# Attention of four gated layers: keys, queries and maxima dealt to stack rows through memory, batches streamed without stages, and in block 0 the clip of the probabilities on GpSimd

## The chip, the cores and the metric

The kernel runs on one core of one Trainium2 chip. The metric is the device time of one execution in microseconds (us). The core has a matrix engine (TensorE, PE), a vector engine (VectorE, DVE), a scalar engine (ScalarE, ACT), a general engine (GpSimd, POOL) and a queue for transfers (SyncE, SP); POOL's queue can issue transfers as well. The engines run their own instruction lists and wait for each other through semaphores.

## The reference, cut to what matters

`x` is 4 batches x 256 tokens x 256 features (D), the context 4 x 512 x 256. Four layers follow each other, each an attention part and a feed-forward part (FFN):

```
x = x + tanh(g_xattn[0]) * L0_xattn(layernorm(x), ctx, mask)   # "block 0": 16 heads of 16
x = x + tanh(g_ffn[0])   * L0_ffn(layernorm(x))                # 8 experts
x = x + tanh(g_xattn[1]) * L1_xattn(layernorm(x), ctx)         # "memory": one head, no weights
x = x + tanh(g_ffn[1])   * L1_ffn(layernorm(x))
x = x + tanh(g_xattn[2]) * L2_xattn(layernorm(x), ctx)         # "block 2": 16 heads, int8 queries
x = x + tanh(g_ffn[2])   * L2_ffn(layernorm(x))                # sign weights
x = x + tanh(g_xattn[3]) * L3_xattn(layernorm(x), ctx, lens)   # "block 3": two softmaxes
x = x + tanh(g_ffn[3])   * L3_ffn(layernorm(x))                # 16 experts
```

Attention of block 0, per batch and head:

```
q, k, v = x @ Wq.T + bq, ctx @ Wk.T + bk, ctx @ Wv.T + bv      # split in 16 heads of 16
scores  = clip(q @ k.T / 4, -50, 50);  masked keys get -50
probs   = softmax(scores);  probs = probs / (sum(probs) + 1e-8)
out     = layernorm(res_scale * ((probs @ v) @ Wo.T + bo)) * gamma + beta
```

Block 2 quantizes its input and its attention output to int8 by the row's largest value; block 3 normalizes queries and keys by their root mean square and has one softmax over the 257 image keys and one over the text keys, whose results are added. Blocks 2 and 3 subtract each row's maximum ahead of the exponential.

## The kernel before, in words

**Precision.** Every fp32 factor of a product is split in a high and a low part, and PE makes three passes (high x high, low x high, high x low). For the scores the parts stand in one "stack" of 64 rows per head: 16 rows of the high part, 16 of the low, 16 of the high again, and 16 for masks and maxima; two heads (a pair) fill the 128 rows. One matmul over the stack does all passes of a score.

**Stacks by turning.** Tokens are projected with tokens on the partitions (`kv`, `q`; the matmuls are at L370). ACT copies the high parts into `stack_k` or `stack_q` (L719), DVE the low parts (L899). PE turns the stack by matmuls with an identity, eight 128x128 for 128 tokens (`turn_stacks`, L541; "tk" for keys, "tq" for queries), and ACT (L750) and DVE (L1057) copy the result out of PSUM into `keys` and `queries`, two buffers each. In blocks 2 and 3 queries are turned a second time ("re") once the maxima stand in the stack (L912, L914).

**Work on a pair.** A unit is one head and 256 keys: `scores` (L596) makes two matmuls of 256 columns into one of two PSUM banks; ACT takes the exponential of 128x512 (L728). 32 units make a batch. In block 0 DVE clips four units' exponentials, 128x2048, to e^-50 and e^50 (L1013; 8 per batch). `weigh` (L634) multiplies by the values, 8 or 12 instructions per four units, each of four passes on fp32. `maxima` (L610) makes a 128x512 product per head and 128 tokens in three banks that the projections use too, and DVE reduces it (L1025 in block 2, L1022 and L1023 in block 3): 32 products per batch.

**The order.** `order` writes down one list of steps, and every engine follows it. It is cut in stages: stage s holds the projections and turns of batch s, the scores of batch s-1 spread over them, the finish of batch s-2 (`dt`, `ot`, `wo`), and at its end the maxima of batch s. Costs in `COST` only set how scores are spread. Blocks 2 and 3 start the scores of a stage after "neg" and "re", which need all maxima of the batch. There are 6 stages for 4 batches. POOL does roots (L765), zeroes the unused halves of `queries` (L783), and splits some weights and contexts.

Of the kernel before, what the change touches and what calls it, by code (L numbers as in the profile page):

```python
# [81 lines left out]
PARTS = 2 * G  # L82


def stage_steps(s, peak):
# [1976 lines left out]
```

How the kernel before makes its waits and increments, by code:

```python
    def wait(eng, kind, n):  # L349
        if isinstance(n, int) and n <= 0:
            return
        eng.wait_ge(sems[kind], n)
# [1 line left out]
    def link(eng, name, ins):  # L355
        chain[name] += 1
        ins.then_inc(sems[name], 1)
        eng.wait_ge(sems[name], chain[name])
# [26 lines left out]
        def w(eng, kind, n):  # L386
            if n > 0:
                eng.wait_ge(sems[kind], n + before_attention("pw" if kind[:2] == "pw" else kind, blk))
# [85 lines left out]
            def kv(b, kt):  # L475
                if b == 0 and kt == 0:
                    if blk == 0:
                        eng.wait_ge(sems["w0_l"], 1)
                        eng.wait_ge(sems["bias_l"], 2)
                    elif blk == 2:
                        eng.wait_ge(sems["w2_l"], 2)
                    else:
                        eng.wait_ge(sems["w3_l"], 6)
                if blk == 0 and kt == 0:
                    eng.wait_ge(sems["ct_l" if b else "ct_l0"], max(b, 1))
                wait_proj_free(eng, b, kt)
# [3 lines left out]
                        mats[m_] = [[(mi, P)], [(mi, P)], [(m_, P), (mi, 1)], [(m_, P)]][kt]  # L490
                lhs = lambda m: ctx_cols(b, kt * P, kt * P + m)
                dst = place(b, kt)
                project(mats[WK], dst, lhs)
                if blk == 0 and b == 0 and kt == 0:
                    eng.wait_ge(sems["w0_l"], 2)
                bank = PROJ_BANKS[(5 * b + PROJ_USE[kt]) % 3]
                then(project(mats[WV], psum[:, bank, D:2 * D], lhs), "pj_full")
# [1405 lines left out]
        def masks():  # L1903
            eng.wait_ge(sems["d_small"], 16 * 5)
```

## Time and profile before

| | |
|---|---|
| time, median of 3 | 1501.76 us (1501.28 to 1501.77) |
| profiled execution | 1505.82 us, span of its trace 1504.0 us |
| mean granted TensorE clock | 0.868 |
| PE busy | 1235.6 us (82%) |
| DVE busy | 868.8 us (58%) |
| ACT busy | 598.5 us (40%) |
| POOL busy | 190.3 us (13%) |
| DMA | 37.16 MB, mean 25 GB/s |

Busy times are sums over the span; every number after this one is on the trace's own clock, which begins at 0 and ends at 1504.0. Block 0 lies from 0 to 262.6, the FFNs and the memory attention to 594.6, block 2 to 886.9, its FFN to 934.0, block 3 to 1257.3, and the last FFN to the end. "Granted clock" is the share of 2.4 GHz that TensorE ran at; a stretch at 0.5 runs at 1.2 GHz.

### The profile page before, as it was taken

Reading aid. Unit: us, or ns where it says so; the run is one execution under the profiler, and the core shown is the slowest. Engines: PE = TensorE matmul, PEld = TensorE weight load, DVE = VectorE, ACT = ScalarE, POOL = GpSimd, SP = SyncE. Lnnn points to the kernel's source line nnn. Section 1 sums busy time; section 2 is a strip of 40 time slices with the busy share of each in tenths; the row PEclk is TensorE's granted clock in tenths of the full one; section 3 lists DMA queues with packets and bytes.
Section 4 is the critical chain, followed back from the end, with each engine's and each line's share of the span. In section 5 each row is a group of like instructions: output and inputs, shape, how many; then the busy total and the mean of one; then the engine's idle time right before and its main releaser. Section 6 shows DMA issues by size and latency. Waiting matters only on the chain. (4 is left out here: it accounts for less than half of the span.)

```text
span 1504.0 us, 21057 instructions
## 1 busy us (share of the span) xinstructions
PE 1235.6 (82%) x7698; PEld 981.6 (65%) x7698; DVE 868.8 (58%) x1890; ACT 598.5 (40%) x1161; POOL 190.3 (13%) x213
## 2 busy tenths in 40 slices
PE   3887874899856997688888767788888876999998
PEld 3765642788745886565656545565757556888887
DVE  6455465455567456667586656567474724555555
ACT  3555642233222232234535533335545351333332
POOL 6000001222101122000000030300001001222221
PEclk8898886799968899569889889769798986999999
DMA  3000001111010010000000020000000001111111
GB/s 128 1 1 1 1 1 58 67 49 49 22 51 14 25 56 6 0 1 1 1 1 1 1 84 25 1 1 1 1 1 1 1 1 38 49 49 53 57 49 40
DMA packets 17925, 37.16 MB, mean 25 GB/s; under 512 B 2341, under 2 KB 7734, under 8 KB 17850
## 3 DMA queue, kind: packets, MB, share of 16 engines
q1 hardware_dynamic: 17690, 36.14, 7.6%
q8 instruction: 48, 0.79, 0.2%
q14 instruction: 27, 0.22, 0.1%
q0 software_dynamic: 160, 0.01, 0.0%
HBM read 35.10 MB, written 1.05 MB: 24 GB/s over the span
## 5 line engine op out<-in xcount | busy, mean ns | idle before, releaser
L728 ACT ACTIVATE probs<-psum 128x512 f32<-128x512 f32 x384 | 218.1, 600 | 188.9 <-PE psum L596 183.2
L596 PE MATMUL psum<-queries,keys 128*128 128x256 f32 x768 | 170.0, 329 | 25.4 <-ACT probs L728 25.1
L1406 DVE TENSOR_TENSOR ff_hl<-ff_h,ff_hh 128x512 fp32r<-128x512 f32 x114 | 108.4, 951 | 139.5 <-ACT ff_hh L1263 139.5
L370 PE MATMUL psum<-ff_xh,ff_wh 128*128 128x512 f32 x424 | 171.1, 404 | 2.1 <-DVE ff_xl L1378 1.4
L596 PEld LDWEIGHTS psum<-queries,keys 128*128 128x128 f32 x768 | 128.6, 212 | 67.5 <-ACT probs L728 53.4
L370 PE MATMUL psum<-ff_xl,ff_wh 128*128 128x512 f32 x424 | 169.6, 400 | 0.0
L1287 ACT ACTIVATE ff_s<-psum 128x512 f32<-128x512 f32 x98 | 58.7, 599 | 250.5 <-PE psum L370 250.5
L370 PE MATMUL psum<-ff_xh,ff_wl 128*128 128x512 f32 x392 | 154.9, 395 | 0.0
L610 PE MATMUL psum<-keys,queries 128*128 128x512 f32 x256 | 126.1, 554 | 19.8 <-DVE negmax L1025 10.1
L370 PE MATMUL psum<-ff_wh,ff_hh 128*128 128x256 f32 x456 | 128.3, 286 | 7.8 <-DVE ff_hl L1406 7.7
L634 PE MATMUL psum<-probs,values 128*32 128x256 f32 x1664 | 124.4, 427 | 9.0 <-DVE probs L1013 6.6
L370 PE MATMUL psum<-ff_wh,ff_hl 128*128 128x256 f32 x456 | 126.8, 283 | 0.0
L370 PE MATMUL psum<-ff_wl,ff_hh 128*128 128x256 f32 x392 | 110.9, 283 | 0.0
L541 PE MATMUL psum<-ident_r,stack_k 128*128 128x128 f32 x384 | 67.4, 327 | 48.9 <-DVE stack_k L899 40.6
L610 PEld LDWEIGHTS psum<-keys,queries 128*128 128x128 f32 x256 | 54.1, 222 | 76.2 <-DVE negmax L1025 34.3
L370 PEld LDWEIGHTS psum<-ff_wh,ff_hh 128*128 128x128 f32 x456 | 86.8, 190 | 18.1 <-DVE ff_hl L1406 13.3
L1388 DVE TENSOR_TENSOR ff_s<-ff_s,psum 128x512 f32<-128x512 f32 x98 | 66.8, 682 | 54.5 <-PE psum L370 54.5
L541 PEld LDWEIGHTS psum<-ident_r,stack_k 128*128 128x128 f32 x384 | 60.9, 239 | 56.2 <-DVE stack_k L899 46.0
L370 PEld LDWEIGHTS psum<-ff_xh,ff_wh 128*128 128x128 f32 x424 | 82.5, 194 | 17.3 <-DVE ff_xl L1378 1.8
L370 PEld LDWEIGHTS psum<-ff_xl,ff_wh 128*128 128x128 f32 x424 | 82.4, 194 | 13.2
L370 PE MATMUL psum<-w_hi,ctx_hi 128*128 128x256 f32 x208 | 68.8, 331 | 23.0 <-DVE bias L1898 12.8
L370 PEld LDWEIGHTS psum<-ff_wh,ff_hl 128*128 128x128 f32 x456 | 86.9, 191 | 0.1
(246 smaller groups left out, 2419.5 us busy)
## 6 DMA issues: line engine op xcount, KB each, us to landing
ff_raw<-in_ff SPq DMA_DIRECT2D x49, 448.0 KB, 3.3
w_raw<-in_w SPq DMA_DIRECT2D x12, 256.0 KB, 4.4
ff_raw<-in_ff SPq DMA_DIRECT2D x8, 256.5 KB, 2.7
ct_raw<-in_ctx_t SPq DMA_DIRECT2D x4, 512.0 KB, 7.5
cn_raw<-in_ctx SPq DMA_DIRECT2D x4, 512.0 KB, 5.2
x<-in_x SPq DMA_DIRECT2D x4, 256.0 KB, 7.4
out<-x SPq DMA_DIRECT2D x8, 128.0 KB, 1.8
w_nat<-in_w_nat SPq DMA_DIRECT2D x1, 512.0 KB, 5.5
```

The source lines that it names most:

```text
L370: last = eng.matmul(dst, lhs[i](k), rhs[j](k), start=start and n == 0, stop=stop and n == groups * len(pairs) - 1, skip_group_check=True)
L541: last = eng.matmul(psum[:, bank, j * P:(j + 1) * P], src[:, 4 * h + j, :], ident_r[:, :], start=True, stop=True, skip_group_check=True)
L596: last = eng.matmul(psum[:, n % 2, i * S:(i + 1) * S], kst[c % 2][:, h // 2, kt * P:(kt + 1) * P], qst[c % 2][:, h % 2, h // 2, :], start= ...
L610: last = eng.matmul(psum[:, PROJ_BANKS[n % 3], :], qst[b % 2][:, h % 2, h // 2, qt * P:(qt + 1) * P], kst[b % 2][:, h // 2, :], start=True ...
L634: last = eng.matmul(psum[32 * j:32 * j + 32, 4, col:col + S], values[:, c % 2, slot, h * VW:h * VW + 32], probs[:, n % 3, j, kt * S:(kt + ...
L728: then(eng.activation(probs[:, n // 4 % 3, u % 4, :], psum[:, n % 2, :], ACT.Exp, scale=SCALE), "p_exp")
L1287: then(eng.activation(ff_s[:, hf, :], psum[:, 4 + hf, :], ACT.Silu), "f_sd")
L1388: then(eng.tensor_tensor(ff_s[:, hf, :], ff_s[:, hf, :], psum[:, 6, :], ALU.mult), "f_td")
L1406: then(eng.tensor_tensor(ff_hl[:, hf, :], ff_h[:, hf, :], ff_hh[:, hf, :].bitcast(F32), ALU.subtract), "f_hr")
```

## The change

- Keys are projected already turned in blocks 0 and 2 (`kt`: features on partitions, 512 keys in a row, six matmuls of 512 columns per half); the weights' columns are put in a fitting order on the host, and the bias comes with ACT's copy (`bias_c`). Block 3 projects two tiles of tokens into one bank (`kp`) and turns them with four transposes (`tk`); queries of blocks 2 and 3 likewise (`tq`).
- High and low parts go to `keys_turned` and `queries_turned`. SP writes them to DRAM (`keys_out` 3 x 512 KB per batch, `queries_out` 3 x 256 KB), and POOL's queue reads them back into the stack rows, in two halves of 8 heads each (`kr`, `qr`: four pieces of 48 rows x 8 KB, four of 64 rows x 4 KB per batch). The constant rows come from DRAM once per buffer; the mask of block 0 is the exponential's bias.
- Maxima are reduced into `nmx`, cast, turned by one matmul per half (`nt`), written to DRAM and read into the query rows (`nr`); no second turning of the queries.
- A unit is one pair and 128 keys, one matmul of 512 columns. Block 0 has three score banks.
- No stages: `order` gives each step a position counted in units, over all batches; blocks 2 and 3 make one maximum per unit, and its scores come 23.5 units later (`LAG`).
- In block 0 POOL clips (`cl`), and DVE no longer does.

```diff
-COST = {"kv": 2.0, "xt": 0.8, "neg": 0.5, "re": 1.8, "kn": 0.3, "st": 0.6, "tk": 1.7, "q": 1.5, "dt": 1.0,
-        "ot": 0.8, "tq": 1.8, "ln": 0.8, "wo": 1.2, "mx": 1.25, "early": 4.0}
...
-        if peak and s < B:
-            stage += [("mx", s, h) for h in range(NH)]
...
+LAG = 23
+SCORE_BANKS = {0: (0, 1, 2), 2: (0, 1), 3: (0, 1)}
...
+        if peak:
+            for k in range(UNITS_OF_BATCH):
+                at(r + k, "mx", c, k)
...
+        for u in range(UNITS_OF_BATCH):
+            at(r + u + lag + .5, "sc", c, u)
+        for part in range(PARTS):
+            if not peak:
+                at(r + 4 * part + 3 + 1.4, "cl", c, part)
...
+            def keys_turned(st):
...
+                then(passes(eng, bank(st), parts(WK, slice(m * P, (m + 1) * P)), ctx_cols(b, 0, M)), "b_full")
...
-                    for j in range(4):
-
-                        last = eng.matmul(psum[:, bank, j * P:(j + 1) * P], src[:, 4 * h + j, :], ident_r[:, :],
-                                          start=True, stop=True, skip_group_check=True)
...
-                for i in range(2):
-                    kt = 2 * (part % 2) + i
-                    last = eng.matmul(psum[:, n % 2, i * S:(i + 1) * S],
-                                      kst[c % 2][:, h // 2, kt * P:(kt + 1) * P],
-                                      qst[c % 2][:, h % 2, h // 2, :], start=True, stop=True,
-                                      skip_group_check=True)
...
+                dst = psum[:, score_banks[n % len(score_banks)], :].rearrange("p (h c) -> p h c", c=S)
+                then(eng.matmul(dst, kst[buf(c)][:, pair, kt * P:(kt + 1) * P], qst[buf(c)][:, :, pair, :],
+                                start=True, stop=True, skip_group_check=True), "st_full")
...
+            def keys_in(b, ph):
+                wait_buffer(b, ph)
+                eng.wait_ge(sems["d_kw"], written(b))
+                pairs = slice(JJ * ph, JJ * (ph + 1))
+                for m in range(2):
+                    src = kd[b, m, :, :, pairs, :].rearrange("s r j c -> (s r) j c")
+                    move(kst[buf(b)][64 * m:64 * m + AUG, pairs, :], src, f"d_r{buf(b)}{ph}")
...
+            def clip(c, part):
+
+                n = PARTS * c + part
+                w(eng, "p_exp", 4 * (n + 1))
+                pr = probs[:, n % 3, :, :, :].rearrange("p k j c -> p (k j c)")
+                then(eng.tensor_scalar(pr, pr, EXP50N, EXP50P, ALU.max, ALU.min), "p_done")
...
+            def keys_out(b):
+                w(eng, "lo_done", plan.count["lo_done", ("te" if two else "ke", b, 1)])
+                for slot, half in enumerate((1, 0, 1)):
+                    move(kd[b, :, slot].rearrange("m r j c -> (r j) m c"), kt_st[:, :, half, :].bitcast(F32), "d_kw")
```

PE's list before, in block 2 when batch 1 is prepared (L541 are turns, L596 scores of batch 0, L610 maxima of batch 1, L634 weighted sums):

```order
L541 MATMUL psum<-ident_r,stack_k 128x128 x8
L596 MATMUL psum<-queries_60,keys_52 128x256 x4
L610 MATMUL psum<-keys_53,queries_61 128x512 x2
L596 MATMUL psum<-queries_60,keys_52 128x256 x2
L610 MATMUL psum<-keys_53,queries_61 128x512 x2
L634 MATMUL psum<-probs,values 32x256 x8
L596 MATMUL psum<-queries_60,keys_52 128x256 x2
L610 MATMUL psum<-keys_53,queries_61 128x512 x4
L596 MATMUL psum<-queries_60,keys_52 128x256 x2
L610 MATMUL psum<-keys_53,queries_61 128x512 x2
L596 MATMUL psum<-queries_60,keys_52 128x256 x4
```

and after, in the same block (L688 are maxima, L679 scores, L712 weighted sums, L632 turns the maxima):

```order
L712 MATMUL psum<-probs,values 32x256 x8
L688 MATMUL psum<-keys_53,queries_60 128x512
L679 MATMUL psum<-queries_60,keys_53 128x512
L688 MATMUL psum<-keys_53,queries_60 128x512
L679 MATMUL psum<-queries_60,keys_53 128x512
L688 MATMUL psum<-keys_53,queries_60 128x512
L679 MATMUL psum<-queries_60,keys_53 128x512
L688 MATMUL psum<-keys_52,queries_59 128x512
L679 MATMUL psum<-queries_60,keys_53 128x512
L712 MATMUL psum<-probs,values 32x256 x8
L632 MATMUL psum<-ident_r,nm_hl 128x128
```

The turns are gone, a unit's scores are one instruction, and maxima alternate with scores one to one over the whole batch, also across its end.

DVE's list before at the same place, the batch's maxima (L1025) in one piece:

```order
L826 RECIPROCAL small<-small 128x1
L827 TENSOR_SCALAR xn<-xn,small 128x256
L828 TENSOR_SCALAR xn<-xn 128x256
L1057 CAST keys_53<-psum 128x4x128
L1025 TENSOR_REDUCE negmax<-psum 128x1 x32
L952 TENSOR_SCALAR xt_hi<-psum 128x512
L912 CAST stack_q<-negmax 128x16 x2
L914 TENSOR_TENSOR stack_q<-negmax,stack_q 128x16 x2
L1057 CAST queries_61<-psum 64x4x128 x2
```

and after (L1139 are the maxima; L1023 to L1036 the norm of a coming batch's input):

```order
L1139 TENSOR_REDUCE nmx<-psum 128x1 x12
L1023 BN_STATS stat<-x 128x6 x2
L1026 BN_AGGR mv<-stat 128x2 x2
L1028 TENSOR_SCALAR ve<-mv 128x2
L1139 TENSOR_REDUCE nmx<-psum 128x1 x2
L1036 TENSOR_SCALAR xn<-x,mv,rstd 128x256 x2
L1003 TENSOR_REDUCE small<-xn 128x2
L1004 TENSOR_SCALAR small<-small 128x2
L1005 RECIPROCAL small<-small 128x2
L1007 TENSOR_SCALAR xn<-xn,small 128x256 x2
L1010 TENSOR_SCALAR xn<-xn 128x512
L1139 TENSOR_REDUCE nmx<-psum 128x1 x2
```

The 32 reductions now come in pieces with the norm, the key parts and the small casts between them.

POOL's list before, block 0 (L783 zeroes, L765 roots, L1157 the norm ahead of the FFN):

```order
L765 ISA
L765 TENSOR_TENSOR rstd<-ve,half_neg 128x2
L1828 TENSOR_TENSOR ctx_lo<-ct_raw,ctx_hi 128x2x512 x3
L783 MEMSET queries_60 64x2048
L783 MEMSET queries_61 64x2048
L783 MEMSET queries_60 64x2048
L783 MEMSET queries_61 64x2048
L765 TENSOR_TENSOR rstd<-ve,half_neg 128x2 x6
L1157 TENSOR_TENSOR rstd<-ve,half_neg 128x6
```

and after, part of block 0 (L944 are clips, L897 reads back keys and queries, L888 roots):

```order
L944 TENSOR_SCALAR probs<-probs 128x2048 x5
L888 TENSOR_TENSOR rstd<-ve,half_neg 128x2
L944 TENSOR_SCALAR probs<-probs 128x2048 x4
L897 DMA keys_53<-keys_out 48x2048 x2
L897 DMA queries_60<-queries_out 64x1024 x2
L888 TENSOR_TENSOR rstd<-ve,half_neg 128x2
L944 TENSOR_SCALAR probs<-probs 128x2048
L897 DMA keys_53<-keys_out 48x2048 x2
L897 DMA queries_60<-queries_out 64x1024 x2
L944 TENSOR_SCALAR probs<-probs 128x2048 x3
```

Clips stand between the transfers' issues and the roots; a transfer that waits for its data holds what is behind it.

## Rows read from the trace of the kernel before

**Rows 1.** Windows: stretch, us; busy PE, PEld, DVE, ACT, POOL; clock; DMA share, GB/s.
```profile
0.00:262.60 262.60, 182.03 (x1370) 139.80 (x1370) 143.72 (x306) 125.79 (x240) 32.04 (x35) 0.84 0.08 27
262.60:594.60 332.00, 286.52 (x1558) 249.18 (x1558) 186.39 (x379) 103.88 (x191) 55.66 (x57) 0.89 0.12 39
594.60:886.90 292.30, 229.89 (x1482) 166.01 (x1482) 191.49 (x427) 124.82 (x238) 12.91 (x12) 0.81 0.02 5
886.90:934.00 47.10, 36.91 (x198) 28.70 (x198) 31.34 (x50) 16.69 (x41) 11.19 (x11) 0.90 0.19 57
934.00:1257.30 323.30, 263.75 (x1778) 190.47 (x1778) 186.67 (x533) 142.56 (x297) 29.22 (x52) 0.84 0.01 4
1257.30:1504.00 246.70, 236.53 (x1312) 207.43 (x1312) 129.21 (x200) 84.78 (x154) 49.29 (x49) 0.96 0.15 47
```
**Rows 2.** Windows: one batch's stage in block 2, a later one, one in block 3.
```profile
657.70:715.60 57.90, 49.40 (x357) 35.38 (x357) 37.38 (x80) 31.45 (x59) 0.70 (x1) 0.90 0.00 1
776.00:836.20 60.20, 51.75 (x380) 37.58 (x372) 41.05 (x86) 30.76 (x59) 0.00 (x0) 0.91 0.00 1
999.00:1065.00 66.00, 56.12 (x426) 41.49 (x426) 42.89 (x125) 37.04 (x78) 5.39 (x13) 0.92 0.00 1
```
**Rows 3.** One line's instructions: L912, L728, L1013 (min/median/max ns; starts).
```profile
L912 DVE CAST stack_q<-negmax x16: 173/176/184, 657.7 to 1196.4; 128x16 fp32r<-128x16 f32 x8, 128x32 fp32r<-128x32 f32 x8
...
L728 ACT ACTIVATE probs<-psum x384: 579/597/667, 50.7 to 1238.7; 128x512 f32<-128x512 f32 x192
...
L1013 DVE TENSOR_SCALAR probs<-probs x32: 1215/1227/1228, 53.6 to 239.1; 128x2048 f32<-128x2048 f32 x32
```
**Rows 4.** Page, costliest groups: exponentials (L728), turns (L541).
```profile
L728 ACT ACTIVATE probs<-psum 128x512 f32<-128x512 f32 x384 | 218.1, 600 | 188.9 <-PE psum L596 183.2
...
L541 PE MATMUL psum<-ident_r,stack_k 128*128 128x128 f32 x384 | 67.4, 327 | 48.9 <-DVE stack_k L899 40.6
```
**Rows 5.** Timeline of PE: turns, scores, weighted sums.
```profile
659.36 1.01 PE L541 MATMUL psum<-ident_r,stack_q 128*128 128x128 f32 x8
...
1234.52 0.74 PE L596 MATMUL psum<-queries,keys 128*128 128x256 f32 x4
...
1237.11 1.07 PE L634 MATMUL psum<-probs,values 128*32 128x256 f32 x16
```
**Rows 6.** Chain of waits in FFN3: 12 matmuls of 512 columns, 12 of 256.
```profile
1402.72 4.18 PE psum L370 x24
```
**Rows 7.** Groups of DVE in 657.7 to 715.6 (block 2).
```profile
L1025 DVE TENSOR_REDUCE negmax<-psum 128x1 f32<-128x512 f32 x32 | 19.6, 683 | 3.0 <-PE psum L610 3.0
L1057 DVE CAST queries<-psum 64x512 fp32r<-64x512 f32 x8 | 5.5, 687 | 5.5 <-PE psum L541 5.4
L1057 DVE CAST keys<-psum 128x512 fp32r<-128x512 f32 x4 | 2.8, 690 | 2.2 <-PE psum L541 2.2
```
**Rows 8.** Timeline of DVE: first maxima of block 2 and of block 3.
```profile
633.53 19.22 DVE L1025 TENSOR_REDUCE negmax<-psum 128x1 f32<-128x512 f32 x32
...
972.45 0.41 DVE L1022 TENSOR_REDUCE negmax<-psum 128x1 f32<-128x257 f32 x1
```
**Rows 9.** Groups of POOL over the program.
```profile
L783 POOL MEMSET queries<- 64x2048 f32 x12 | 21.6, 1829 | 0.3
...
L1836 POOL CAST w_hi<-w_raw 128x512 fp32r<-128x512 f32 x8 | 5.5, 684 | 0.1
```
**Rows 10.** DMA of 0 to 50 us (16 engines' share); issues of the page.
```profile
q1 hardware_dynamic: 3624, 4.82, 28.8%
...
ct_raw<-in_ctx_t SPq DMA_DIRECT2D x4, 512.0 KB, 7.5
```
**Rows 11.** Timeline near 15 us and at 971 us: DVE L844, POOL L1828.
```profile
15.22 4.81 DVE L844 TENSOR_SCALAR xn<-x,mv,rstd 128x256 f32<-128x256 f32 x2 [0.84 <-POOL rstd L765]
...
971.20 0.73 DVE L844 TENSOR_SCALAR xn<-x,mv,rstd 128x256 f32<-128x256 f32 x2 [0.82 <-POOL rstd L765]
...
15.18 7.08 POOL L1828 TENSOR_TENSOR ctx_lo<-ct_raw,ctx_hi 128x1024 fp32r<-128x1024 f32 x3
```

More of the change, by code:

```diff
@@ new lines, in token_pair @@
+            def token_pair(st, mat, img):
+                _, b, i = st
+                if b == 0 and i == 0:
+                    wait_weights(mat)
+                wait_bank(eng, st)
+                for k in range(2):
+                    kt = 2 * i + k
+                    mats = [(mat, P)]
+                    if two:
+                        mats = [[(img, P)], [(img, P)], [(mat, P), (img, 1)], [(mat, P)]][kt]
+                    last = project(mats, bank(st)[:, k * D:(k + 1) * D],
+                                   lambda m: ctx_cols(b, kt * P, kt * P + m))
+                then(last, "b_full")
@@ new lines, in keys_hi @@
+            def keys_hi(st):
+                _, b, i = st
+                if b and i == 0:
+                    eng.wait_ge(sems["d_kw"], written(b - 1))
+                if blk != 3:
+                    fill = ("kt", b, i)
+                    filled(eng, fill)
+                    then(eng.activation(kt_st[:, i, 1, :], bank(fill), ACT.Identity, bias=key_bias(i)), "hi_done")
+                else:
+                    fill = ("tk", b, i)
+                    copy_hi(st, fill, kt_st[:, :, 1, 2 * P * i:2 * P * (i + 1)],
+                            bank(fill).rearrange("p (m c) -> p m c", m=2))
@@ new lines, in turned_lo @@
+            def turned_lo(st, fill, hi, lo):
+                flat = lambda t: t[:, :, :].rearrange("p c t -> p (c t)")
+                if blk == 2:
+                    wait_readers(eng, st, ("q", "wo"))
+                    filled(eng, fill)
+                    ins = eng.tensor_scalar(flat(hi), bank(fill), -127.0, None, ALU.max)
+                else:
+                    w(eng, "hi_done", plan.count["hi_done", st])
+                    ins = less(flat(lo), bank(fill), flat(hi))
+                then(ins, "lo_done")
@@ new lines, in divide @@
+                dst = o if part == 0 else o_tmp[:, :].rearrange("p (h c) -> p h c", c=HD)
+                spread = inv.rearrange("p (h one) -> p h one", one=1).to_broadcast([P, NH, HD])
+                ins = eng.tensor_tensor(dst, got[:, :, 0:HD], spread, ALU.mult)
+                then(ins, "dt_done")
+                w(eng, "dt_done", plan.count["dt_done", st])
+                last = qt == QT - 1 and part == nparts - 1
+                if blk == 2 and last:
+                    then(quantize(o_n, o_slot(b)), "on_done")
+                elif two and part == 1:
+                    ins = eng.tensor_tensor(o_n[:, qt, :], o_n[:, qt, :], o_tmp[:, :], ALU.add)
+                    if last:
+                        then(ins, "on_done")
@@ L1999, in units @@
         return m.transpose(1, 0, 2).reshape(D, -1)
+    turned = np.array([(2 * j + m) * HD + r for m in range(2) for r in range(HD) for j in range(NP)])
     arrays = {}
```

1283 lines of the change are left out of this document (713 added, 570 removed), and 17 rows, old and new, of the table PREP.

## The prediction, as put on record before the changed kernel ran

> **What bounds the kernel now.** I read first the windows of the whole program [rows 1]. The attention parts of blocks 0, 2 and 3 take 262.6, 292.3 and 323.3 us, together 878.2 of 1504.0. The rest (332.0 + 47.1 + 246.7 = 625.8 us) keeps its arithmetic, so I leave it as it is. In the attention parts PE is busy for 69%, 79% and 82%, at a granted clock of 0.84, 0.81 and 0.84; the last FFN, where PE is busy for 96% of the window, has 0.96. DVE is busy for 55%, 66% and 58% there, ACT for less than half. PE is the main engine, but something else stops it.
>
> Next one batch at a time. The casts of the maxima (L912) of block 2 start at 657.7 and the last batch's at 836.2: (836.2 - 657.7)/3 = 59.5 us per batch; in block 3 (1196.4 - 999.0)/3 = 65.8; in block 0 first exponential to last clip is (239.1 - 50.7)/4 = 47.1 [rows 2, 3]. A stage of block 2 holds 49.4 to 51.8 us of busy PE at clock 0.90 and 0.91, one of block 3 56.1 at 0.92 [rows 2]; the sum of the instructions at full clock is 42 and 48 us (below), so a batch takes 1.4 times what its matmuls need. The page says why: exponentials (L728) were idle for 188.9 us behind PE's scores, and the turns (L541) for 48.9 us behind the stacks that ACT and DVE fill [rows 4]. Last, the maxima stand in one piece: 32 reductions in 19.22 us, 0.60 us each, in the first batch of block 2 [rows 8], during which PE can't run ahead by more than three banks.
>
> **Unit prices at full clock.** Eight turning matmuls 1.01 us; four score matmuls of 256 columns 0.74 by the record, of which the last's end is modelled; 16 records of weighted sum 1.07 [rows 5]. 12 matmuls of 512 columns and 12 of 256 take 4.18 us [rows 6]: by columns 0.232 and 0.116 us each.
>
> **Part 1, PE.** Per batch of block 2 before: maxima 32 x 0.232 = 7.4, scores 64 x 0.116 = 7.4, sums 8 x 1.07 = 8.6, turns 64 matmuls (32 for keys, 16 + 16 for queries) in 8 groups x 1.01 = 8.1, projections 72 x 0.116 = 8.3, transposes 16 and the like 2.2: 42. After: the 8.1 are gone, four transposes (0.5) and two small turns of maxima (0.2) come, scores are 32 x 0.232 = 7.4 as before, and the keys' bias matmuls (4) go: 34. Block 3 by the same count: 48 before; after -8.1 + 1.5 = 41.5. Block 0 has 48 turns per batch (6.1 us): 34 before, 27.5 after. Over 12 batches that is 85 us less of PE. Scores become half as many instructions with the same columns, which I cost at nothing for PE: their columns set their time; the semaphores halve.
>
> **Part 2, DVE and ACT.** In block 2 DVE loses 12 copies of 0.69 us per batch (8 of queries, 4 of keys) [rows 7] and about six low parts of 0.4, and gets three of 0.69 and two small casts: 41.05 - 8.3 - 2.5 + 2.7 = 33 us per batch; block 3: 42.9 - 8.1 = 35 [rows 2]. That stays under PE. In block 0 the clip goes: 8 x 1.227 = 9.8 us per batch [rows 3]. ACT loses copies likewise and stays near 25 us per batch. What hid the reductions in block 2's end-of-stage piece, nothing, is replaced by one reduction per unit beside a score and an exponential (0.60) [rows 3].
>
> **Part 3, the trip through memory.** Per batch 1536 KB of keys go out and 1536 KB come in, queries 768 KB out and 1024 KB in: 4.98 MB. In the first 50 us 4.82 MB took 28.8% of 16 engines, that is 335 GB/s if all work; a single load of 512 KB took 7.5 us, 70 GB/s [rows 10]. So a batch costs 15 to 71 us of the transfer engines, otherwise idle (share 0.01 to 0.08 [rows 1]). I take 20 us: the pieces are kilobytes long and three or four of them are under way together, as in the first 50 us. The order writes keys 26 units ahead of their first use and reads them 17, over 25 us for one write and one read (7.5 us each), so from the second batch the trip is hidden; if the cover is gone a block's first batch alone pays it, about 12 us. SP has nothing else to do in these stretches. POOL's queue holds the reads behind clips and, in block 2 and 3, behind the roots: a read that waits for its data delays the roots queued behind it, and DVE's norm with them; the norm stands 30 units ahead, which covers it.
>
> **Part 4, the clip on POOL.** No tensor_scalar of 2048 columns on POOL is in the trace. From below: zeroing 2048 columns took 1.829 us; from the middle a one-input cast of 512 took 0.684, four times 2.7 us [rows 9]; from above, two-input subtractions of 1024 columns, three in 7.08 us, 2.3 ns per column, so 4.7 us [rows 11]. The clip has one input, so I take 2.7. POOL per batch of block 0: 8 x 2.7 + 8 issues of about 0.6 + roots 1.4 = 28 us, under the 32 forecast below; at 4.7 it is 44.
> Of one-input work the trace has only the cast. The Trainium skill ("GPSIMD Engine Reference", section 3.1) puts bodies of up to two operations at 1.03 cycles per element at 1.2 GHz and two inputs at 2.6; by it the clip would be, as an estimate, 1.8 us, and the trace's two prices per column (1.3 and 2.3 ns) stand in that order.
>
> **The pace after.** PE's work divided by a clock of 0.88 (the windows had 0.81 to 0.92), plus some waits: block 0 27.5/0.88 = 31, I take 32; block 2 34/0.88 = 38.6, I take 41; block 3 41.5/0.88 = 47, I take 48.
> - Block 0: first exponential at 40 (50.7 now; fewer steps stand ahead of it, a trip of 12 is added), 4 x 32 = 128, tail 20 (23.5 now: 262.6 - 239.1): 188.
> - Block 2: first maxima at 25 (39 now: 633.53 - 594.6 [rows 8]; six tiles need not be stacked and turned first), 23 units of maxima alone 24, 105 units of both at 41/32 = 134, the last 23 units of scores alone 20, finish 14: 217.
> - Block 3: 30 (38 now: 972.45 - 934.0 [rows 8]) + 25 + 105 x 1.5 = 157 + 20 + 18: 250.
> Sum 655 against 878: -223, span 1281. The timed median stands 2.2 us under the profiled span (1501.76 against 1504.0; the profiled execution itself 1505.82). **Predicted: 1279 us.**
>
> **Rivals.**
> - *POOL is the bound of block 0.* If the clip takes 4.7 us, a batch takes 44 us instead of 32: +48, 1327. For it: two-input work does take that [rows 11]; against: the clip has one input. 15%.
> - *DVE is held beside the clips.* At 15.22 two small DVE operations took 4.81 us beside POOL's subtraction, at 971.20 0.73 [rows 11]. If every clip holds DVE for its length, DVE needs in block 0 its own 14 us (143.72/4 less 9.8 and copies) + 22 = 36 per batch: +16, 1295. Much of DVE's work there reads PSUM. 12%.
>  The Trainium skill ("SBUF — State Buffer", "Who interferes with whom") says VectorE and GpSimd share a port pair that one of them locks for a whole instruction, against operations in fast modes or with two SBUF inputs; the 4.81 against 0.73 us agree.
> - *The coupling stays.* PE still waits at two score banks for ACT's exponential and at two or three for DVE, and the ratio of 1.4 to its work stays: 38.5, 47.6, 58 us per batch, +26, +22, +33: 1360. For it: those waits are in the scores' rows now [rows 4]; against: half as many handshakes, and no stage ends. 13%.
> - *PE runs unbroken* at a clock near the 0.96 of the last FFN: 29, 36, 43.5 per batch and shorter leads: 1279 - 12 - 17 - 15 - 10 = 1225. 10%.
> - *Slower than before: memory paces it.* If each piece crawls like the 512 KB load at 70 GB/s and one follows the other, 71 us per batch: 12 x 71 + 135 of leads and tails + 626 = 1613. It is the bound from about 45 us per batch on and makes the kernel slower above (878 - 135)/12 = 62 us, an effective rate under 80 GB/s. Against: 335 GB/s when several are under way [rows 10]. 3%.
> - *It doesn't do what it says*: the buffers' reuse or a late read serialises batches, so nothing is won in blocks 2 and 3 and block 0 alone gains. 2%: about 1430.
>
> **Chances.** The forecast has the remaining 45%, its own range 1245 to 1315. 8 in 10 is 1215 to 1360: below it half of the unbroken case, above it part of the coupled, the serial and the memory case. This kernel's runs differ by 0.03%, so 0.2% (3 us) can be told from no change. All cases but the memory one are faster by far more: faster 0.96, within 0.2% 0.01, slower 0.03.
>
> **What would show it.** Right: no turning matmuls between stages; one maximum and one score alternating every 1.3 to 1.5 us in blocks 2 and 3; casts of maxima 41 and 48 us apart per batch; block 0 from 262.6 to near 188; the clip near 2.7 us with POOL under 90% busy; scores never idle behind the read-back after the first batch. Wrong: scores or maxima that wait for a transfer in batches 1 to 3 (memory), POOL full in block 0, DVE operations of 3 to 5 us beside clips, or PE idle behind exponentials and reductions as often as before at a clock still under 0.85.

## The result, and the profile after

The changed kernel takes 1552.59 us (median of four, 1545.94 to 1557.38) against 1501.76: a ratio of 1.0327, 95% interval 1.0281 to 1.0372. It is slower by 3.3%. The forecast was 1279 us, with 0.03 for slower. The profiled execution has a span of 1550.0 us.

Page, busy times and granted clock in 40 slices:

```profile
PE 1138.5 (73%) x6554; PEld 844.9 (55%) x6554; DVE 842.4 (54%) x1588; ACT 520.8 (34%) x997; POOL 480.9 (31%) x365
...
PEclk7756766655899886997688997876979997999999
```

PE is busy for 97 us less than before (the forecast took 85 us of work from it), but its clock is 0.5 to 0.7 of full speed in the first ten slices, and GpSimd is busy for 481 us instead of 190.

Windows of the changed kernel, cut at the same events as [rows 1] (the last norm ahead of each FFN, the stores of `x` that end it); columns as there:

```profile
0.00:377.50 377.50, 186.08 (x978) 113.16 (x978) 190.09 (x211) 112.25 (x192) 278.47 (x103) 0.65 0.34 76
377.50:709.30 331.80, 286.16 (x1558) 248.90 (x1558) 186.34 (x379) 103.81 (x191) 55.63 (x57) 0.90 0.13 40
709.30:951.60 242.30, 174.38 (x1059) 107.41 (x1059) 151.89 (x318) 93.31 (x178) 36.51 (x62) 0.84 0.43 94
951.60:998.70 47.10, 37.80 (x198) 29.28 (x198) 30.99 (x50) 16.70 (x41) 11.19 (x11) 0.90 0.18 57
998.70:1302.60 303.90, 217.08 (x1450) 138.33 (x1450) 153.90 (x434) 110.01 (x241) 49.82 (x86) 0.85 0.35 75
1302.60:1550.00 247.40, 237.06 (x1312) 207.83 (x1312) 129.23 (x200) 84.75 (x154) 49.29 (x49) 0.96 0.15 47
```

The three FFN stretches kept their times (331.8, 47.1, 247.4 against 332.0, 47.1, 246.7). Block 0 went from 262.6 to 377.5 us, block 2 from 292.3 to 242.3, block 3 from 323.3 to 303.9: +115, -50, -19. All of the loss is in block 0. The forecast for the three was 188, 217 and 250, so it was out by 189, 25 and 54 us.

Three groups of the page: the clips, the scores and block 2's maxima:

```profile
L944 POOL TENSOR_SCALAR probs<-probs 128x2048 f32<-128x2048 f32 x32 | 226.5, 7079 | 29.9 <-ACT probs L851 27.7
...
L679 PE MATMUL psum<-queries,keys 128*128 128x512 f32 x384 | 177.6, 498 | 36.0 <-DMA queries<-maxima_out 28.8
...
L1139 DVE TENSOR_REDUCE nmx<-psum 128x1 f32<-128x512 f32 x128 | 82.8, 684 | 50.4 <-PE psum L688 49.9
```

The clip (L944) took 7.08 us, where 2.7 was forecast with 4.7 as the upper bound. By line, minimum, median and maximum in ns with first and last start, clips and the exponentials of block 0:

```profile
L944 POOL TENSOR_SCALAR probs<-probs x32: 7064/7070/7205, 76.5 to 346.0; 128x2048 f32<-128x2048 f32 x32
...
L851 ACT ACTIVATE probs<-psum,aug x128: 677/687/728, 65.2 to 338.6; 128x512 f32<-128x512 f32 x128
```

The minimum is 7.064 and the median 7.070, so nearly all of the 32 take the same time, whatever runs beside them. 32 clips in (346.0 - 76.5)/31 = 8.7 us each make 70 us a batch, against 47.1 before [rows 3]. The first exponential is at 65.2, where 50.7 stood before and 40 was forecast. GpSimd's timeline in the second batch:

```profile
164.35 7.07 POOL L944 TENSOR_SCALAR probs<-probs 128x2048 f32<-128x2048 f32 x1 [4.45 <-ACT probs L851]
171.48 1.13 POOL L897 DMA_DIRECT2D keys<-keys_out  x2
172.60 1.06 POOL L897 DMA_DIRECT2D queries<-queries_out  x2
173.67 0.74 POOL L888 TENSOR_TENSOR rstd<-ve,half_neg 128x2 f32<-128x2 f32 x1
174.50 7.07 POOL L944 TENSOR_SCALAR probs<-probs 128x2048 f32<-128x2048 f32 x1
181.64 1.12 POOL L897 DMA_DIRECT2D keys<-keys_out  x2
182.75 1.05 POOL L897 DMA_DIRECT2D queries<-queries_out  x2
183.88 21.50 POOL L944 TENSOR_SCALAR probs<-probs 128x2048 f32<-128x2048 f32 x3
```

Of the 70 us of a batch, 57 are its eight clips, about 4.5 the eight issues of read-backs (0.55 us each) and 1 to 2 the roots. The rest is mostly idle time in which a clip waits for its exponentials (29.9 us over the block, in the group's row). The weighted sums, and with them what stands behind them on PE, wait for the clips: 92.4 us in PE's matmuls (L712).

A second loss is on VectorE. The three norms of tokens ahead of the first FFN, six instructions, in the changed kernel beside clips:

```profile
338.76 15.71 DVE L1382 TENSOR_SCALAR ff_xn<-x,mv,rstd 128x256 f32<-128x256 f32 x6 [1.47 <-POOL rstd L1368]
```

and in e5 below, which differs in that VectorE does the clips and in the start:

```profile
210.43 2.02 DVE L1382 TENSOR_SCALAR ff_xn<-x,mv,rstd 128x256 f32<-128x256 f32 x6 [1.44 <-POOL rstd L1368]
```

2.6 us each against 0.34; the longest of these norms takes 7.27 us, about the length of a clip. VectorE is busy for 190 us in block 0 of the changed kernel and for 121 in e1 below, although e1 has 39 us of clips on it. So about 109 us of VectorE's busy time in block 0 come with the clips on GpSimd. The Trainium skill ("SBUF — State Buffer", "Who interferes with whom") says that VectorE and GpSimd share a port pair, which one of them can hold for a whole instruction while the other stands; the trace agrees with it: 15.71 against 2.02 us.

### The profile page after: what moved, and what is told of

The parts are those of the page before. It is cut to its first block and busy times, and to the rows that moved or that the text cites. A ratio compares the mean times of both kernels' runs of the same rounds, so it can differ in the third digit from the quotient of the medians.

```text
span 1550.0 us, 18481 instructions
## 1 busy us (share of the span) xinstructions
PE 1138.5 (73%) x6554; PEld 844.9 (55%) x6554; DVE 842.4 (54%) x1588; ACT 520.8 (34%) x997; POOL 480.9 (31%) x365
## 5 line engine op out<-in xcount | busy, mean ns | idle before, releaser
L944 POOL TENSOR_SCALAR probs<-probs 128x2048 f32<-128x2048 f32 x32 | 226.5, 7079 | 29.9 <-ACT probs L851 27.7
L853 ACT ACTIVATE probs<-psum 128x512 f32<-128x512 f32 x256 | 145.2, 598 | 189.2 <-PE psum L679 186.6
L712 PE MATMUL psum<-probs,values 128*32 128x256 f32 x1664 | 137.6, 462 | 94.3 <-POOL probs L944 92.4
L679 PE MATMUL psum<-queries,keys 128*128 128x512 f32 x384 | 177.6, 498 | 36.0 <-DMA queries<-maxima_out 28.8
L688 PE MATMUL psum<-keys,queries 128*128 128x512 f32 x256 | 125.5, 506 | 16.0 <-DVE nmx L1137 5.7
L712 PEld LDWEIGHTS psum<-probs,values 128*32 128x32 f32 x1664 | 51.3, 125 | 155.6 <-issue 90.8
L679 PEld LDWEIGHTS psum<-queries,keys 128*128 128x128 f32 x384 | 82.5, 226 | 95.9 <-DMA queries<-maxima_out 32.2
L851 ACT ACTIVATE probs<-psum,aug 128x512 f32<-128x512 f32 x128 | 80.2, 689 | 118.9 <-PE psum L679 118.6
L1139 DVE TENSOR_REDUCE nmx<-psum 128x1 f32<-128x512 f32 x128 | 82.8, 684 | 50.4 <-PE psum L688 49.9
L1563 POOL TENSOR_TENSOR ff_wl<-ff_raw,ff_wh 128x512 fp32r<-128x512 f32 x49 | 63.2, 1290 | 136.9 <-ACT ff_wh L1486 136.9
L1566 POOL TENSOR_TENSOR ff_wl<-ff_raw,ff_wh 128x256 fp32r<-128x256 f32 x49 | 36.2, 740 | 222.4 <-ACT ff_wh L1492 222.4
L1136 DVE TENSOR_REDUCE nmx<-psum 128x1 f32<-128x257 f32 x128 | 53.9, 421 | 89.9 <-PE psum L688 89.1
```

Source lines behind the costliest of these rows:

```text
L679: then(eng.matmul(dst, kst[buf(c)][:, pair, kt * P:(kt + 1) * P], qst[buf(c)][:, :, pair, :], start=True, stop=True, skip_group_check=True ...
L688: then(eng.matmul(bank(st), qst[buf(b)][:, m, pair, qt * P:(qt + 1) * P], kst[buf(b)][:, pair, :], start=True, stop=True), "mx_full")
L712: last = eng.matmul(psum[32 * j:32 * j + 32, SUM_BANK, col:col + S], values[:, c % 2, slot, h * VW:h * VW + 32], probs[:, n % 3, i, j, :], ...
L851: ins = eng.activation(dst, src, ACT.Exp, scale=SCALE, bias=aug0[:, KT * c + kt:KT * c + kt + 1])
L853: ins = eng.activation(dst, src, ACT.Exp, scale=SCALE)
L944: then(eng.tensor_scalar(pr, pr, EXP50N, EXP50P, ALU.max, ALU.min), "p_done")
```

## The experiments

Theory 1 was that the clip on GpSimd sets the pace of block 0. The rivals were the trip through memory, GpSimd's queue with its read-backs, and the start.

**e1, clips back on VectorE** (everything else as changed):

```diff
 # pool()
-                elif st[0] == "cl":
-                    clip(st[1], st[2])
 # dve()
+                elif st[0] == "cl":
+                    clip(st[1], st[2])
```

> The changed kernel with the clips of block 0 back on VectorE. Theory 1, the clip on GpSimd paces block 0: its 32 clips took 7.07 us each and started 8.7 us apart, so without them a batch falls from 70 to 32-38 us and the kernel from 1552 to about 1410 (1385 to 1430), faster than the 1502 of before. Rival, transfers pace block 0 (its transfer engines were busy for a share of 0.34) or the late start does: the pace stays near 60 us per batch and the time above 1500.

1413.03 us, ratio 0.9415 to before (0.9381 to 0.9449). Block 0 takes 239.8 us, the others are as in the changed kernel (241.7, 304.0). The part of the change that moves the clip costs 140 us; the rest of the change gains 88 us on the kernel before. Block 0's window and its exponentials:

```profile
0.00:239.80 239.80, 143.30 (x978) 91.00 (x978) 120.62 (x243) 110.89 (x192) 55.16 (x71) 0.81 0.52 120
...
L851 ACT ACTIVATE probs<-psum,aug x128: 679/689/779, 65.1 to 212.5; 128x512 f32<-128x512 f32 x128
```

(212.5 - 65.1)/4 = 36.9 us per batch. Theory 1 holds. PE's clock in the block is 0.81 instead of 0.65, and the same 978 matmuls keep it busy for 143 us instead of 186.

**e2, the kernel before with the clips on GpSimd**, the same edit in the other kernel:

> The kernel before with only the clips of block 0 on GpSimd. Theory 1, the 7.07 us belong to the instruction: the same 7.07 us, GpSimd needs 57 us and its roots per batch against 47 us now, block 0 longer by 40 to 60 us, about 1550. Rival, the 7.07 us come from new neighbours (transfers issued by the same engine, the read-backs): a clip of 2 to 3 us and block 0 shorter than before, about 1490.

The clips, and the window of block 0:

```profile
L777 POOL TENSOR_SCALAR probs<-probs x32: 7068/7071/7090, 54.8 to 344.1; 128x2048 f32<-128x2048 f32 x32
...
0.00:375.20 375.20, 201.30 (x1370) 153.35 (x1370) 235.93 (x274) 126.24 (x240) 258.24 (x67) 0.73 0.06 19
```

1618.35 us (one run), block 0 375.2 us instead of 262.6. The duration comes with the instruction: 7.07 us with no read-back in the kernel. The loss of 113 us was twice what I expected. I had counted GpSimd alone; VectorE, without the 39 us of clips, is busy for 236 us in the block instead of 144, 131 us more than its own work took before, and PE stood 61.8 us for the `stack_k` that VectorE fills (before: 22.6).

**e3, four forms of the operation**, one per batch, upper bound or clip left out in two of them:

```diff
-                then(eng.tensor_scalar(pr, pr, EXP50N, EXP50P, ALU.max, ALU.min), "p_done")
+                if c == 0: ins = eng.tensor_scalar(pr, pr, EXP50N, EXP50P, ALU.max, ALU.min)
+                elif c == 1: ins = eng.tensor_scalar(pr, pr, EXP50N, None, ALU.max)
+                elif c == 2:   # two pieces of 1024
...
+                else: ins = eng.tensor_scalar(pr, pr, 1.0, 0.0, ALU.mult, ALU.add)
```

> The changed kernel, clips on GpSimd in four forms, one per batch: both bounds over 2048 columns; the lower bound alone; both bounds in two pieces of 1024; multiply by one and add zero. Batches 1 and 3 leave the clip or one of its bounds out. If the price is by operation and column, 7.07 us, about 3.6 us, 2 x 3.55 us, and 7.07 us. If it is a fixed price per instruction, all near 7 us and the two pieces 14. If it is a price of max and min only, the fourth form takes 2 to 3 us.

Groups of POOL:

```profile
L945 POOL TENSOR_SCALAR probs<-probs 128x2048 f32<-128x2048 f32 x8 | 56.6, 7071 | 0.6
...
L947 POOL TENSOR_SCALAR probs<-probs 128x2048 f32<-128x2048 f32 x8 | 43.1, 5387 | 6.4 <-ACT probs L851 6.4
...
L949 POOL TENSOR_SCALAR probs<-probs 128x1024 f32<-128x1024 f32 x8 | 29.0, 3623 | 1.6 <-ACT probs L851 1.0
...
L952 POOL TENSOR_SCALAR probs<-probs 128x2048 f32<-128x2048 f32 x8 | 15.4, 1928 | 9.2 <-ACT probs L851 9.1
```

Both bounds 7.07, the lower bound alone 5.39, a piece of 1024 columns 3.62, multiply and add 1.93 us. None of the three expectations fits all four. The price goes by column, a second bound adds 1.7, and one pair of operations is 3.7 times cheaper. In the last batch stand multiply and add; their first and last start:

```profile
L952 POOL TENSOR_SCALAR probs<-probs x8: 1892/1905/2082, 259.3 to 289.6; 128x2048 f32<-128x2048 f32 x8
```

They start (289.6 - 259.3)/7 = 4.3 us apart. In the same batch the clips start 8.5 us apart in the changed kernel and 4.5 in e1, where VectorE makes them. So work of this kind on GpSimd, in the same place of its queue, doesn't slow the batch; the clip's length does, with what it holds on VectorE. This is one batch of one run, and in none of the three kernels are read-backs issued in it.

**e8, four more forms:** upper bound alone (L945), multiply alone (L947), lower bound then multiply (L949), multiply then lower bound (L951).

> The changed kernel, GpSimd's operation on the probabilities by batch: upper bound alone; multiply by one alone; lower bound then multiply; multiply then lower bound. Bounds are left out in every batch. In the run with four forms both bounds took 7.07 us, the lower bound alone 5.39, multiply and add 1.92. If max and min are dear on GpSimd: 5.4, about 1.9, 5 to 6, 5 to 6 us. If an instruction of a single operation is dear: 5.4, 5.4, 2 and 2.

```profile
L949 POOL TENSOR_SCALAR probs<-probs 128x2048 f32<-128x2048 f32 x8 | 56.8, 7096 | 6.8 <-ACT probs L851 6.3
...
L951 POOL TENSOR_SCALAR probs<-probs 128x2048 f32<-128x2048 f32 x8 | 56.7, 7082 | 5.9 <-ACT probs L851 5.3
...
L947 POOL TENSOR_SCALAR probs<-probs 128x2048 f32<-128x2048 f32 x8 | 43.1, 5396 | 8.1 <-ACT probs L851 8.1
...
L945 POOL TENSOR_SCALAR probs<-probs 128x2048 f32<-128x2048 f32 x8 | 42.9, 5370 | 0.0
```

5.37, 5.40, 7.10, 7.08 us. Both expectations fell. A single multiply costs as much as a single max; only multiply with add is fast. In these eight rows every other form pays 2.6 ns per column for one operation and 3.45 for two. Why isn't shown.

**e4, tokens first in the queue of loads** (on e1; the queries' weights move ahead likewise):

```diff
+        load(x[:, 0:QT, :], x_rows[0], "d_x0")
         for b in range(B):
             src = a["aug_q"].rearrange("r (one c) -> one r c", one=1)
             load(qd[b, :, 3].rearrange("m r j c -> m r (j c)"), src.to_broadcast([2, HD, NP * S]), "d_aq")
-        load(x[:, 0:QT, :], x_rows[0], "d_x0")
```

> As the first kernel, and the tokens of batch 0 and the queries' weights are loaded ahead of the four writes of constant rows instead of behind them. Theory: the first exponential of the changed kernel is at 65.2 us because the tokens landed 22.6 us after their issue; it comes at about 50, so 10 to 15 us faster than the first kernel. Rival: the trip of keys and queries through memory sets that start, which the order of loads leaves alone: within 4 us of the first kernel.

1417.36 us (ratio 0.9445, 0.9419 to 0.9470): nothing gained. VectorE's and then GpSimd's timeline show why:

```profile
11.07 0.17 DVE L1019 TENSOR_SCALAR ve<-mv 128x2 f32<-128x2 f32 x1
30.61 3.86 DVE L1027 TENSOR_SCALAR xn<-x,mv,rstd 128x256 f32<-128x256 f32 x2 [19.37 <-POOL rstd L888]
...
28.61 1.10 POOL L897 DMA_DIRECT2D keys<-in_aug_k  x2 [19.59 <-DMA queries_out<-in_aug_q]
29.81 0.76 POOL L888 TENSOR_TENSOR rstd<-ve,half_neg 128x2 f32<-128x2 f32 x1
```

The tokens' variance is ready at 11.24. Its root comes at 29.81, since GpSimd's queue stood 19.59 us in front of it, on the writes of constant rows (19.0 us in the changed kernel). The norm (L1027) then starts at 30.61 and takes 3.86 us beside GpSimd's zeroing.

**e5, that wait moved to the first read of queries** (on e4):

```diff
-            else:
-                eng.wait_ge(sems["d_aq"], 16 * B)
...
             def queries_in(b, ph):
+                if blk == 0 and b == 0 and ph == 0:
+                    eng.wait_ge(sems["d_aq"], 16 * B)
```

> VectorE clips, tokens first, and GpSimd waits for the constant query rows only ahead of its first read of queries instead of at its start. Theory: in the run before the tokens' sums were ready at 11.1 us, but the root of the norm came at 29.8, queued on GpSimd behind a wait of 19.6 us for the constant rows' writes; with the wait moved the first turned tokens come 15 us earlier, the first exponential near 50, and the time is 8 to 15 us under the 1413 to 1417 of the two runs. Rival: the constant rows are needed for the first scores anyway (first read of queries) and nothing moves by over 3 us.

1411.86 us (0.9385, 0.9349 to 0.9421): within the interval of e1. The norm came early, at 11.5, but the first exponential only at 62.8: ACT's queue now stood 16.3 us on the biases, which land behind the same writes. My theory of e4 had named one of two queues behind one cause.

**e6, read-backs issued by SyncE:** `keys_in`, `queries_in` and `maxima_in` move to SyncE's list (the destinations are named as fp32, with the same bits), on e5:

```diff
 # pool()
-                elif st[0] == "kr":
-                    keys_in(st[1], st[2])
...
 # sp()
+                elif st[0] == "kr":
+                    keys_in(st[1], st[2])
```

> As e5_late, with all read-backs (keys, queries, maxima) issued from SyncE's queue instead of GpSimd's. Theory, the trip's length matters in the leads and for each batch's maxima: reads of 384 and 256 KB took 6.5 and 7.3 us to land from GpSimd's queue, writes of 512 KB 4.2 from SyncE's, so each lead and each wait for maxima gets 2 to 3 us shorter and GpSimd's roots wait for no read: 10 to 25 us faster than e5_late. Rival, the trip is covered or one queue for both directions makes writes wait behind reads: same or slower by up to 10.

1384.38 us (0.9196, 0.9165 to 0.9228), 27 us less. Of my two reasons one fell: the reads didn't land sooner (7.0 and 7.2 us for 384 and 256 KB, against 6.6 and 7.4 in e5). The other held: in the profiled executions block 0 gains 22 us (215.8 against 238.2) with its first exponential at 62.8 in both. In e5 GpSimd's queue stood, in each of two batches, 9 us for the free buffer that a read of queries needs, and the root of an output norm behind it held VectorE. VectorE's wait for these roots (e5 from 85 to 185, e6 from 85 to 165; total, times, longest), and PE's wait in e5 for constant key rows that are issued behind read-backs there (e6 has no such wait):

```profile
DVE o_n L1195 <- POOL rstd L888: 11.4, 2, 5.8
...
DVE o_n L1157 <- POOL rstd L888: 1.6, 2, 0.8
...
PE psum L679 <- DMA keys<-in_aug_k: 6.7, 1, 6.7
```

These are 16.5 us less of waiting, most of the 22. Block 2 got 8 us longer and block 3 7 us shorter, which I can't explain. Exponentials of block 0 in e6:

```profile
L851 ACT ACTIVATE probs<-psum,aug x128: 680/691/775, 62.8 to 188.6; 128x512 f32<-128x512 f32 x128
```

(188.6 - 62.8)/4 = 31.5 us per batch; the forecast had 32. It is a mean: the first batch takes 24, the two in the middle 35 to 37.

**e7, scores 27.5 units behind the maxima** (`LAG = 27`, otherwise e5):

> As e5_late with scores 27.5 units behind the maxima instead of 23.5 in blocks 2 and 3. Theory, PE stands for the maxima's trip (28.8 us in matmuls of the changed kernel, up to 8.6 us at a time): the four units more cover 5 us of each, 10 to 20 us saved less 7 us for a longer tail: 3 to 13 us faster. Rival, those waits only stand in for work that is late anyway (projections, transfers): 4 to 8 us slower by the longer tail.

1376.11 us (0.9136, 0.9099 to 0.9173), 36 us less than e5. PE's waits for the maxima, e5 and then e7 (total, times, longest):

```profile
PE psum L679 <- DMA queries<-maxima_out: 28.4, 7, 7.5
```

```profile
PE psum L679 <- DMA queries<-maxima_out: 10.7, 4, 5.8
```

Block 2 fell from 238.7 to 227.1 and block 3 from 305.4 to 288.6 us. The waits explain 18 us of the 28; the rest isn't in rows that I can name.

**e9, e10: both, constant rows written last, lag 27 and 29:**

```diff
-LAG = 23
+LAG = 27      # e10: 29
...
         for b in range(1, B):
             context_and_tokens(b)
+        for b in range(B):   # writes of constant rows
```

> VectorE clips, read-backs from SyncE's queue, scores 27.5 units behind, and the constant query rows written last of the first loads. If the parts add: 1384 less the 35 us that the longer lag gave, so about 1350, and up to 12 less because in e5_late the biases landed at 28 us behind the constant rows and held the scalar engine for 16 us: 1338 to 1350. Rival: lag and queue removed the same waits for maxima: 1360 to 1370.

> As e9_best27 with scores 29.5 units behind. Theory, 10.7 us of PE's waits for maxima were left at 27.5: 0 to 6 us faster. Rival, the rest of the waits are not the trip's and the tail grows by two units in two blocks: 2 to 4 us slower.

1345.76 us (0.8982, 0.8951 to 0.9014) and 1338.48 us (0.8924, 0.8904 to 0.8944). e9 gives what e6 and e7 gave apart, and e10 is 7 us faster, a little more than its 0 to 6. In e10 the casts of the maxima are 36.8 us per batch apart in block 2 and 49.4 in block 3, from 44.8 and 58.0 in e5 (first to last of the eight casts, 3.5 batches); the forecast had 41 and 48. The first exponential stays at 61.1 (e9; 62.8 in e5), so next to nothing came of the up to 12 us at the start. SyncE's queue in e9:

```profile
24.77 15.78 SPq L1217 DMA_DIRECT2D queries_out<-queries_turned  x3
```

Three issues that take about 1.5 us elsewhere took 15.78. The constant rows' writes had been issued 11 us earlier; in e13, which has no such writes, the same three issues take 1.46.

**e11, GpSimd's zeroing after the first norm** of blocks 2 and 3:

```diff
                     w(eng, "pw_out", n)
+                    w(eng, "xn_done", 1)
                     zero_queries(eng, 0)
```

> As e9_best27, and in blocks 2 and 3 GpSimd zeroes the unused query halves only after VectorE's first norm. Theory, the two norm instructions that took 3.86 us beside the zeroing and 0.73 elsewhere were held by it: 0.75 us again and 5 to 6 us less in all. Rival, the norm is held by something else or the delay is covered: no change (within 2 us).

Block 3's first norm in e9:

```profile
824.41 3.86 DVE L989 TENSOR_SCALAR xn<-x,mv,rstd 128x256 f32<-128x256 f32 x2 [0.83 <-POOL rstd L888]
```

and in e11:

```profile
827.93 0.73 DVE L990 TENSOR_SCALAR xn<-x,mv,rstd 128x256 f32<-128x256 f32 x2 [0.83 <-POOL rstd L888]
```

3.86 us became 0.73, in block 2 0.74, and the first maxima come 2.9 and 3.9 us sooner. The total is unchanged (1344.02, 0.8972, 0.8936 to 0.9008, against e9's 1345.76): block 3 gained 4 us and block 2 lost 4. So the zeroing did hold the norm, but what that is worth in the total can't be told.

**e12, every write of keys twice** (on e9):

```diff
+                for slot, half in enumerate((1, 0, 1)):
+                    move(kd2[b, :, slot].rearrange("m r j c -> (r j) m c"), kt_st[:, :, half, :].bitcast(F32),
+                         "d_again")
```

> As e9_best27, with every write of keys done a second time to memory that nothing reads: 1.57 MB more per batch, 18.9 MB in all, some 50 us of the 16 transfer engines at the 361 GB/s of the writes. If transfers pace the leads or the batches, each of the 12 batches gets 2 to 4 us longer and the time 20 to 50 us; if their share of the time is covered once the batches run, only the three leads pay, 5 to 15 us.

1372.34 us (0.9135, 0.9116 to 0.9155), 27 us over e9: block 0 +7, block 2 +10, block 3 +15 in the profiled executions. The hardware queue (q1) moved 116.63 MB instead of 97.75, and its share of the 16 engines rose from 27.2% to 29.9%. PE's matmuls stood 33.8 us for read-backs of maxima and queries instead of 13.3. The edit also makes ACT wait for the second copies before it writes the next keys. So 18.9 MB more, with that wait, cost 27 us, 1.4 us per MB, at a total share of 0.3. What the trip's own traffic costs the run doesn't show.

**e13, e14: constant rows straight from the input, then with e11's edit:**

```diff
-            load(qd[b, :, 3].rearrange("m r j c -> m r (j c)"), src.to_broadcast([2, HD, NP * S]), "d_aq")
...
+                        move(qst[buf(b)][64 * m + AUG:64 * m + 64, m, pairs, :],
+                             a["aug_q"].rearrange("r (j c) -> r j c", c=S)[:, pairs, :], f"d_k{buf(b)}{ph}")
```

> As e10_best29, but the constant query rows come straight from the input (once per buffer in block 0, with each batch in blocks 2 and 3) and the four writes of 256 KB through memory are gone. Theory, the transfer engines are the limit of the start (share 0.85 in the first 31 us of e9_best27, SyncE's queue stood 15.8 us on one issue behind those writes): the first exponential comes at 45 to 52 instead of 61 and the time is 8 to 15 us under e10_best29. Rival, the start is held by the chain of contexts and weights alone: within 3 us.

> As e13_nowrite29, with GpSimd's zeroing of unused query halves in blocks 2 and 3 after the first norm: leads of both blocks 3 us shorter as in e11_best27_zero, 3 to 6 us under e13_nowrite29 if it adds, no change if the batches swallow it.

1320.88 us (0.8799, 0.8774 to 0.8823) and 1316.37 us (0.8755, 0.8734 to 0.8775). Exponentials of block 0 in e13:

```profile
L853 ACT ACTIVATE probs<-psum,aug x128: 677/689/778, 46.4 to 169.3; 128x512 f32<-128x512 f32 x128
```

The first comes at 46.4 instead of 60.8, and block 0 is 198 us long instead of 213.7. The theory holds, and the gain (17.6 us) is a little more than its 8 to 15. With the start freed e14 is 4.5 us faster than e13, but their intervals touch, so the edit's own worth stays open. e14 is the fastest kernel here, 12.5% under the kernel before.

**e15, e10 with the clips on GpSimd again:**

> As e10_best29, with the clips of block 0 on GpSimd as in the changed kernel, and no read-back in its queue. Theory, the clip itself is the bound: 8 x 7.08 us and a root or two are 58 us per batch, block 0 is 61 + 232 + 20 = 313 us against 214, the time about 1438. Rival, the queue with transfers between the clips made it slow: clips still 7.07 us, but block 0 under 280.

```profile
L914 POOL TENSOR_SCALAR probs<-probs 128x2048 f32<-128x2048 f32 x32 | 226.6, 7081 | 49.0 <-ACT probs L851 47.1
...
L914 POOL TENSOR_SCALAR probs<-probs x32: 7065/7072/7203, 63.8 to 316.6; 128x2048 f32<-128x2048 f32 x32
```

1471.00 us (one run), block 0 348.0 against e10's 213.7. With no read-back between the clips they cost 134 us there, and the rival falls. The queue and the start, which e15 has otherwise than the changed kernel, make the other 29 of that kernel's 377.5. The time is 33 us over my 1438: a batch takes (316.6 - 63.8)/31 x 8 = 65 us and not 58, since of the 49 us that GpSimd idled for exponentials 25 lie ahead of the first clip and the others between clips.

## Why the prediction was wrong

**Part 4, the clip, is the step that failed.** It gave 2.7 us and, as upper bound, 4.7. It measured 7.07, and with that GpSimd's 28 us per batch, which were to stay under PE's 32, became 63 in a batch of 70. The three rows behind it [rows 9, 11] were a zeroing, a cast and a subtraction, and I took "one input" as what sets the price. e3 and e8, all with one input, show that the operations change it by 3.7 times: multiply with add 1.93 us, close to my lower bound, and every form with a max or min or a single operation 5.4 to 7.1. The quoted rule of the Trainium skill ("GPSIMD Engine Reference", section 3.1), 1.03 cycles per element up to two operations, gave as an estimate 1.8 us; it fits multiply with add (1.93) and not the clip (7.07). The measurement decides. No price for that form was in the trace, and the bounds should have been wider, or the case "GpSimd is the bound" likelier than 15%. That rival named the mechanism and the place; its price was 4.7 instead of 7.07 and its time 1327 instead of 1552.

**Rival 2, VectorE held beside the clips, happened too.** I gave it 36 us of VectorE per batch (14 of its own, 22 held); the windows show 190/4 = 47.5, of which 109/4 = 27 held, so its own work is 20 and not 14. What the holding costs in time can't be told from the clip's length here, since both went with the same edit in e1.

**Part 1, PE, agrees with the runs.** The turns went. Two batches of block 2 in e10:

```profile
630.60:706.50 75.90, 68.90 (x500) 43.54 (x500) 59.81 (x121) 42.45 (x84) 0.70 (x1) 0.98 0.43 99
```

68.90/2 = 34.5 us of PE per batch at a clock of 0.98; the forecast had 34. In block 0 of e6 it is 30.9 at 0.98 (61.86 for two batches), 3 more than the 27.5. The pace came near the forecast only in the repaired kernels: 31.5 us (forecast 32) in e6, 36.8 and 49.4 (forecast 41 and 48) in e10. The changed kernel's own casts of maxima are 45.8 and 57.9 us per batch apart.

**Part 3, the trip, had about the right volume, too short a length, and one trip missing.** The transfers of 60 to 90 us in the changed kernel:

```profile
q0 software_dynamic: 756, 3.57, 73.5%
q1 hardware_dynamic: 1632, 2.36, 21.8%
```

Reads moved 3.57 MB in 22.1 us of engine time (162 GB/s), writes 2.36 MB in 6.5 (361). A batch's 4.98 MB so take 16.2 + 6.5 = 22.7 us; the forecast had 20. But it gave the trip ahead of a block only 12. In block 3 the first keys are written at 1025.3 and the first maximum comes at 1045.9, in block 2 at 724.8 and 745.3: 20.6 and 20.5 us. In block 3's stretch the 16 transfer engines have no idle time (share 1.04 by this view):

```profile
1025.30:1045.90 20.60, 11.26 (x66) 9.95 (x66) 8.30 (x23) 4.69 (x16) 7.54 (x14) 0.73 1.04 242
```

"Hidden from the second batch" is borne out for keys and queries so far as PE's waits show: none of the changed kernel's is for their read-backs. The forecast left out two things. The maxima's own trip, with 23.5 units to cover it, had no term, and PE's matmuls stood 28.8 us for it (shorter in e7 and e10). And the reads in GpSimd's queue held roots that VectorE needed (11.4 us over two batches of e5's block 0). I had called such waits covered, with the norm of the coming batch in mind; it was the norm of the output that was held. Slack counted in units of the plan shrinks with the units.

**The leads.** Block 0's first exponential came at 65.2, not 40: the constant rows' writes through memory held three queues in turn (e4, e5, e9), and without them it is 46.4 (e13). I had those writes in view and gave them no price. Blocks 2 and 3 needed 35.9 and 47.1 us to the first maxima, not 25 and 30; 8.5 us of each miss are the trip's length; the rest I can't name.

**The clock** followed the pace. Two stretches of block 2, early and late:

```profile
745.30:785.70 40.40, 26.70 (x115) 19.14 (x116) 24.10 (x49) 8.07 (x14) 6.97 (x13) 0.71 0.77 148
882.30:917.60 35.30, 32.51 (x249) 19.39 (x241) 27.34 (x54) 21.14 (x42) 2.04 (x4) 1.00 0.01 3
```

The clock is 0.71 where PE is busy for 66% of the stretch, and 1.00 where it is busy for 92%. The forecast divided all work by 0.88; block 0 of the changed kernel had 0.65.

**The sum.** Of 269 us of span that the forecast missed, 190 are block 0's: about 138 the clip (block 0 in the changed kernel and in e1), 25 the start, 20 the pace left in e1 (36.9 instead of 32) and 7 its finish. The other 79 are blocks 2 and 3: 28 their leads, 48 their pace (45.8 and 57.9 us a batch instead of 41 and 48), 3 the rest. The forecast also held that 3 us could be told from no change; further executions of the kernel before lay from 1498.48 to 1510.26.

## What to carry to other kernels

Before work goes to GpSimd, find a row with the same operations, not only the same number of inputs: here a two-bound clip cost 3.7 times a multiply-add of the same size, and VectorE was held beside it. When a transfer or a wait is put in an in-order queue, list what stands behind it; one wait for constants delayed first the norm, then the biases, then SyncE's issues. A change of many parts should be taken apart by run: one part of this one hid a gain of 6% (with the repairs 12.5%).
